# First four stages of a gather-and-multiply kernel picked out of whole tables by matmuls with ones and zeros

## Chip, cores and metric

The kernel runs on one core of a Trainium2 chip. The metric is the device time of one execution in microseconds (us), the median of several. All data are fp32, indices int32.

## What is computed

A batch of 2048 rows, each with 32 ids, one for each of 32 tables of 64 columns. The tables have 1000, 1250, 12500 or 125000 rows.

```
e     = stack(tbl_f[ids[:, f]])                      # (2048, 32, 64)
z     = sum(e, axis=-1)                              # (2048, 32)
outer = einsum('bpd,pde,bpe->bp', e[:, I], K, e[:, J])   # the 496 pairs i < j, K is (496, 64, 64)
h     = concat([z, outer, dense_ctx], axis=1)        # 32 + 496 + 16 = 544
h     = relu(h @ W_top1 + b_top1)                    # 512
h     = relu(h @ W_top2 + b_top2)                    # 256
y     = h @ W_top3                                   # (2048, 1)
```

## The kernel before

The batch is cut into NQ = 8 blocks of QB = 256 rows (two tiles of 128). The 32 fields are taken in pairs, from the last to the first: stage `a` of a block holds fields 2(15-a) and 2(15-a)+1, so stage 0 is fields 30 and 31. K is rearranged on the host and stays in SBUF as `k_sb` (8 MB).

The work on each engine is written out by hand, in an order fixed by tables:

- **POOL** gathers. One indirect DMA fetches 128 table rows (one field, one tile) into `gathered`, four a stage, 64 a block (L313 to L331). Four are in flight (`IN_FLIGHT`): before issuing gather k it waits for gather k-4 (`halve`, L302). From block 1 on `halve` also adds the two halves of each row for the sums z.
- **PE** turns a stage into `x_t` (fields along partitions, batch along columns) by two transposes into the one PSUM bank `tr` (`transpose`, L556); **ACT** copies `tr` into `x_t` (`keep_x`, L365). Everything that goes through `tr` goes one after the other: a fill waits until all earlier ones are kept (`free_tr`, `tr_kept`).
- The pairs are computed in 64 steps a block: 32 "even" steps (`multiply`, L635, K times x_t, weights from `k_sb`) and 32 "turned" ones (`multiply_turned`, L652, x_t as weights). DVE multiplies each result in PSUM by the other factor (`product`, L475; `turned_product`, L492). A turned product reads `gathered` directly, four stages (a block of COLS) at a time: the first ones need stages 4 to 7. The even products are summed by PE with a matrix of ones (`reduce`, L667), the turned ones by ACT (L427) or DVE (L521).
- In block 0 the order is: stages 0, 1, 2, even step 0, stages 3, 4, 5, even step 1, stage 6, even step 2, two turned steps (block 1 of stages), even 3 and so on; stage 7 before even step 5, stage 11 before step 12, stage 15 before step 25 (`FIRST_AHEAD`, L145). DVE sums each gathered stage over its 64 columns into `z_nat` (`sum_x`, L463); at the end of the block these are transposed (`sums_of_x`).
- **SP** loads: the ids, three small tensors, K in ten pieces (`K_LOADS`; from the fourth on each waits for a number of copies out of `tr`, L345), then w1 and w2, then for each block the dense columns in and the results out.
- ACT issues no DMA. The three layers on top (L583 to L633) run for block q-1 beside the steps of block q.

`x_t` has two blocks' slots (16 stages each), `z_sb` and `z_nat` two each.

Of the kernel before, what the change touches and what calls it, by code (L numbers as in the profile page):

```python
# [7 lines left out]
P = 128  # L8
NQ = 8
# [12 lines left out]
COLS = 4  # L22
YC = 4
# [98 lines left out]

STAGES_AT_ONCE = [1] + [2] * (NQ - 1)
# [82 lines left out]
def dlrm_tower(nc, ids, tables, kmat, dense_t, w1, b1, w2, b2, w3, out):  # L206
# [6 lines left out]
    with ctx:  # L213
# [23 lines left out]
        y_sb = sb("y_sb", [P, YN])  # L237
        idx = sb("idx", [P, NQ * STAGES * GATHERS], i32)
# [16 lines left out]
        small_loaded = sem("small_loaded")  # L255
        weights_loaded = sem("weights_loaded")
# [20 lines left out]
        LAST = NQ - 1  # L277
        FIRST_K = STAGES * GATHERS
# [14 lines left out]
        @block.gpsimd  # L293
        def _(pool):
            nc.gpsimd.memset(ident[:], 0.0).then_inc(zeroed, 1)
            pool.wait_ge(zeroed, 1)
            nc.gpsimd.affine_select(out=ident[:], in_=ident[:], compare_op=ALU.not_equal, fill=1.0,
                                    base=0, pattern=[[-1, P]], channel_multiplier=1).then_inc(consts_ready, 1)
            pool.wait_ge(idx_loaded, 16)


            def halve(k):  # L302
                G, n = divmod(k, GATHERS)
                t, f = divmod(n, 2)
                pool.wait_ge(gather_landed[k % IN_FLIGHT], (k // IN_FLIGHT + 1) * 16)
                if k < FIRST_K:
                    return
                if n == 0 and G - HR >= STAGES:
                    pool.wait_ge(x_summed, G - HR + 1)
                at = gathered[:, t, G % GR, f * D:(f + 1) * D]  # L310
                nc.gpsimd.tensor_tensor(x_half[:, G % HR, t, f, :], at[:, 0:D // 2], at[:, D // 2:D], ALU.add).then_inc(x_halved, 1)  # L311

            for k in range(NQ * STAGES * GATHERS):  # L313
                G, n = divmod(k, GATHERS)
                q, a = divmod(G, STAGES)
                t, f = divmod(n, 2)
                if k >= IN_FLIGHT:
                    halve(k - IN_FLIGHT)
                if n == 0 and G >= GR:
                    pool.wait_ge(tr_filled, place_of_stage(q - 1, a))  # L320
                    if q == 1:
                        pool.wait_ge(x_summed, G - GR + 1)
# [12 lines left out]
        @block.sync  # L335
        def _(sp):
# [27 lines left out]
        def _(act):  # L364
            def keep_x(q, a):  # L365
# [85 lines left out]
        def _(dve):  # L451
# [63 lines left out]
            def sum_turned(q, i):  # L515
                c, t = divmod(i, TILES)
                dve.wait_ge(prod_ready, q * NS + STEP_OF[q]["turned", i] + 1)
                if q >= 2:
# [4 lines left out]
                                        axis=AX.X, op=ALU.add).then_inc(summed_dve, 1)  # L523

# [23 lines left out]
        def _(pe):  # L548
# [20 lines left out]
            def sums_of_x(q):  # L569
                pe.wait_ge(x_summed, (q + 1) * STAGES)  # L570
# [221 lines left out]
```

## Time and profile before

| | us |
|---|---|
| median of 3 runs | 814.21 (813.42 to 814.73) |
| the profiled execution | 812.35 |
| its span on the core | 810.5 |
| busy: PE, DVE, ACT, POOL | 761.7, 720.8, 681.7, 607.3 |

The page of the profile gives one execution: busy time of each engine, the chain of waits that ended last, groups of instructions by line, and the DMA queues. Windows give the same for chosen stretches. The timeline lists instructions in order of time, like neighbours merged, with the idle time in front of each and who ended it. PE is TensorE's matmuls and PEld its weight loads; a matmul's end is modelled, so the distance from one start to the next says more than the duration. A fp32 matmul appears as two instructions, a transpose as one.

### The profile page before, as it was taken

How to read it: one execution, taken by the hardware profiler on the slowest of the kernel's cores; microseconds unless marked ns; L12 is line 12 of the kernel's file. 1: busy time of each engine (PE TensorE's matmuls, PEld its weight loads, DVE VectorE, ACT ScalarE, POOL GpSimd, SP SyncE). 2: the span in 40 equal slices, each digit the busy share in tenths (PEclk: the TensorE clock that was granted, in tenths of full speed). 3: DMA queues.
4: the chain of work that ended last, by engine and by line, in shares of the span. 5: the costliest groups of instructions: out<-in, count | busy, mean ns of one | idle time of the engine just before them, and what ended most of it. 6: DMA issues, size and time to landing. Idle time of an engine off the chain costs nothing.

```text
span 810.5 us, 20371 instructions
## 1 busy us (share of the span) xinstructions
PE 761.7 (94%) x6000; PEld 458.4 (57%) x6000; DVE 720.8 (89%) x684; ACT 681.7 (84%) x5282; POOL 607.3 (75%) x966
## 2 busy tenths in 40 slices
PE   0378989999999999999999999999999999999998
PEld 0144435565565666666666666656565665656656
DVE  0268999998999989999999989999999999999891
ACT  1057899989979999789989899799997899798993
POOL 6775888888888888888888888888868888660000
PEclk9999999999999999999999999999999999999999
DMA  4545111111111111111111111111111111110000
GB/s 136 162 134 181 27 24 26 25 26 25 26 26 25 26 25 25 26 25 25 25 27 25 25 25 26 25 25 26 24 23 24 26 25 26 20 21 2 1 2 1
DMA packets 20014, 28.74 MB, mean 35 GB/s; under 512 B 9024, under 2 KB 9664, under 8 KB 19008
## 3 DMA queue, kind: packets, MB, share of 16 engines
q0 software_dynamic: 16384, 16.81, 10.7%
q1 hardware_dynamic: 3520, 10.63, 4.0%
q8 instruction: 48, 0.79, 0.4%
q14 instruction: 62, 0.51, 0.2%
HBM read 27.40 MB, written 0.01 MB: 34 GB/s over the span
## 4 chain that ended last, share of the span: by engine, by line
PE 83%; DMA 6%; POOL 6%; issue 2%; ACT 2%; DVE 1%; DVEq 0%; POOLq 0%
PE m_ps L646 25%; PE m_ps L662 25%; PE acc L676 13%; PE tr L585 8%; DMA gathered<-in_tbl,idx 6%; POOL gathered L328 6%; PE tr L566 4%; PE tr L599 3%; ACT turned_act L427 1%; PE m_ps L648 1%; PE m_ps L585 1%; PE tr L580 1%; PE m_ps L599 0%; POOL x_half L311 0%; DMA idx<-in_ids 0%
## 5 line engine op out<-in xcount | busy, mean ns | idle before, releaser
L427 ACT ACTIVATE turned_act<-turned_act 128x64 f32<-128x64 f32 x2560 | 612.1, 244 | 26.3 <-DVE turned_act L513 26.2
L328 POOL DMA_INDIRECT gathered<-in_tbl,idx x512 | 489.4, 956 | 100.2 <-issue 74.4
L427 ACT ACTIVATION_READ_ACCUMULATOR turned_act<-turned_act 128x1 f32 x2560 | 486.4, 190 | 0.0
L488 DVE TENSOR_TENSOR prod<-m_ps,x_t 128x1024 f32<-128x1024 f32 x256 | 308.1, 1217 | 11.2 <-PE m_ps L648 10.7
L646 PE MATMUL m_ps<-x_t,k_sb 64*128 64x256 f32 x1024 | 271.8, 391 | 3.9 <-DVE turned_act L513 2.1
L648 PE MATMUL m_ps<-x_t,k_sb 64*128 64x256 f32 x1024 | 272.6, 392 | 0.0
L662 PE MATMUL m_ps<-k_sb,x_t 64*128 64x512 f32 x1024 | 262.7, 608 | 4.4 <-DVE turned_act L513 3.5
L646 PEld LDWEIGHTS m_ps<-x_t,k_sb 64*128 64x128 f32 x1024 | 182.4, 188 | 107.9 <-issue 63.2
L513 DVE TENSOR_TENSOR turned_act<-m_ps,gathered 128x1024 f32<-128x1024 f32 x160 | 193.4, 1217 | 25.0 <-PE m_ps L662 12.4
L648 PEld LDWEIGHTS m_ps<-x_t,k_sb 64*128 64x128 f32 x1024 | 182.1, 188 | 0.0
L662 PEld LDWEIGHTS m_ps<-k_sb,x_t 64*128 64x128 f32 x1024 | 92.6, 187 | 67.1 <-issue 43.7
L311 POOL TENSOR_TENSOR x_half<-gathered 128x32 f32<-128x32 f32 x448 | 117.2, 262 | 17.4 <-DVE z_nat L472 8.5
L676 PE MATMUL acc<-prod,sel 128*32 128x256 f32 x2048 | 123.6, 382 | 0.0
L513 DVE TENSOR_TENSOR turned_dve<-m_ps,gathered 128x1024 f32<-128x1024 f32 x96 | 117.0, 1219 | 3.2 <-POOL x_half L311 0.5
L521 DVE TENSOR_REDUCE z_turned<-turned_dve 128x16 f32<-128x1024 f32 x96 | 116.1, 1210 | 0.0
L371 ACT ACTIVATE x_t<-tr 128x512 f32<-128x512 f32 (+1 forms) x72 | 39.1, 543 | 66.7 <-PE tr L566 66.7
L676 PEld LDWEIGHTS acc<-prod,sel 128*32 128x32 f32 x2048 | 60.1, 110 | 54.0 <-issue 15.2
L566 PE MATMUL tr<-ident,gathered 128*128 128x128 f32 x256 | 45.3, 296 | 37.1 <-DMA gathered<-in_tbl,idx 37.1
L585 PE MATMUL tr<-z_sb,w_sb 128*128 128x256 f32 x280 | 67.9, 389 | 0.0
L566 PEld LDWEIGHTS tr<-ident,gathered 128*128 128x128 f32 x256 | 27.3, 144 | 70.2 <-issue 33.1
L585 PEld LDWEIGHTS tr<-z_sb,w_sb 128*128 128x128 f32 x280 | 50.9, 190 | 24.6 <-issue 18.8
L463 DVE TENSOR_REDUCE z_nat<-gathered 128x4 f32<-128x256 f32 x16 | 6.7, 416 | 31.8 <-DMA gathered<-in_tbl,idx 31.8
(36 smaller groups left out, 152.6 us busy)
## 6 DMA issues: line engine op xcount, KB each, us to landing
gathered<-in_tbl,idx POOLq DMA_INDIRECT x512, 2.5
k_sb<-in_kmat SPq DMA_DIRECT2D x7, 1024.0 KB, 4.9
w_sb<-in_w SPq DMA_DIRECT2D x1, 1280.0 KB
k_sb<-in_kmat SPq DMA_DIRECT2D x2, 256.0 KB, 3.1
k_sb<-in_kmat SPq DMA_DIRECT2D x1, 512.0 KB, 5.1
w_sb<-in_w SPq DMA_DIRECT2D x1, 512.0 KB
idx<-in_ids SPq DMA_DIRECT2D x1, 256.0 KB, 2.6
z_sb<-in_dense_t SPq DMA_DIRECT2D x8, 16.0 KB, 2.1
```

The source lines that it names most:

```text
L311: nc.gpsimd.tensor_tensor(x_half[:, G % HR, t, f, :], at[:, 0:D // 2], at[:, D // 2:D], ALU.add).then_inc(x_halved, 1)
L328: nc.gpsimd.indirect_dma_start(out=gathered[:, t, G % GR, f * D:(f + 1) * D], out_offset=None, in_=tables[2 * (STAGES - 1 - a) + f], in_of ...
L427: last = nc.scalar.activation(row, row, ACT.Copy, accum_out=z_turned[:, q % 2, t, 16 * c + n:16 * c + n + 1])
L488: nc.vector.tensor_tensor(prod[:, r % PR, :, :].rearrange("p u (e n) -> p u e n", e=2), m_ps[:, p % MR, :, :].rearrange("p u (e n) -> p u ...
L513: nc.vector.tensor_tensor(to, m_ps[:, p % MR, :, :], other, ALU.mult).then_inc(prod_ready, 1)
L521: nc.vector.tensor_reduce(z_turned[:, q % 2, t, 16 * c:16 * c + 16], turned_dve[:, (q * NTD + RANK[i]) % BD, :, :].rearrange("p f (u n) -> ...
L566: last = nc.tensor.transpose(tr[:, c, t * P:(t + 1) * P], gathered[:, t, (G + c) % GR, :], ident[:])
L585: last = nc.tensor.matmul(to, w1_sb[:, b, n * P:(n + 1) * P], z_sb[:, q % 2, b, :], start=(begin and b == blocks[0]), stop=(end and b == b ...
L646: nc.tensor.matmul(m_ps[:, p % MR, 0, n * QB:(n + 1) * QB], k_sb[0:D, at + n, :], x_t[0:D, slot(q, a0), :], start=True, stop=True)
L648: last = nc.tensor.matmul(m_ps[:, p % MR, 1, n * QB:(n + 1) * QB], k_sb[D:P, at + n, :], x_t[D:P, slot(q, a1), :], start=True, stop=True)
L662: last = nc.tensor.matmul(m_ps[:, p % MR, f, :], x_t[f * D:(f + 1) * D, slot(q, m), t * P:(t + 1) * P], k_sb[f * D:(f + 1) * D, at:at + CO ...
L676: last = nc.tensor.matmul(acc[c * 32:c * 32 + 32, 0:QB], sel[:, 30 - 2 * row:62 - 2 * row], prod[:, (q * NE + e) % PR, u, n * QB:(n + 1) * ...
```

## The change

Stages 0 to 3 of block 0 (fields 30 and 31 down to 24 and 25) are no longer gathered. Their tables all have 1000 or 1250 rows, that is 125 x 8 or 125 x 10. Each table is loaded whole, row 125-wise: partition p holds rows p*r to p*r+r-1 (r = 8 or 10), r times 64 columns. The 256 ids of a field are loaded to each of 125 partitions. For each c < r, DVE compares the ids with p*r + c (`rows_sb`), which gives a 125x256 matrix of ones and zeros, and PE multiplies the table's c-th 64 columns by it, adding up in `tr[f*64:(f+1)*64]`: the stage's x_t without a gather or a transpose. There are 18, 18, 16 and 18 such steps in the four stages, 70 in all, through a ring of five matrices (`HOT_RING`).

The loads (13 DMAs: the row numbers, then for each stage the ids and two tables) are issued by ACT at its start. Three stages' tables lie in the part of `x_t` that block 1 uses later; the fourth's and the ring lie in `w1_sb`, so SP's load of w1 now waits for the last pick. The ids lie in `z_sb`. The sums z of the four stages, which DVE took from `gathered`, are eight small matmuls on PE (`first_sums`, kept by ACT), placed before even step 2. POOL's gathers start with stage 4; their counts in all waits are shifted by K0 = 16.

```diff
+HOT = 4
+HOT_P = 125
+HOT_RING = 5
+TABLES_AHEAD = 3
...
+AHEAD[0, FIRST_AHEAD[HOT + 2]].append(("s", 0, 0))
...
+        hot_steps = [(a, c, f) for a in range(HOT) for c in range(max(HOT_R[a])) for f in range(2) if c < HOT_R[a][f]]
+        final = {(a, f): max(j for j, e in enumerate(hot_steps) if e[0] == a) for a in range(HOT) for f in range(2)}
+        used_by = [sum(i != final[hot_steps[i][0], 0] for i in range(j + 1)) for j in range(len(hot_steps))]
...
+        def hot_table(a, f):
+            home, first = (x_flat, 0) if a < TABLES_AHEAD else (w1_flat, TABLES_AHEAD)
+            at = D * (sum(sum(HOT_R[b]) for b in range(first, a)) + (HOT_R[a][0] if f else 0))
+            return home[0:HOT_P, at:at + D * HOT_R[a][f]]
...
-            for k in range(NQ * STAGES * GATHERS):
+            for k in range(K0, NQ * STAGES * GATHERS):
...
+            sp.wait_ge(tr_filled, place("x", 0, HOT - 1))
             sp.dma_start(w1_sb[:], w1.rearrange("(k p) n -> p k n", p=P)).then_inc(weights_loaded, 16)
...
+            act.dma_start(rows_sb[:], rows_hot).then_inc(rows_loaded, 16)
+            for a in range(HOT):
+                act.dma_start(hot_ids(a), ids_hot[a:a + 1, :].rearrange("o (f n) -> o f n", f=2).partition_broadcast(HOT_P)).then_inc(ids_hot_loaded[a], 16)
+                for f in range(2):
+                    act.dma_start(hot_table(a, f), tables[2 * (STAGES - 1 - a) + f].rearrange("(p r) d -> p (r d)", p=HOT_P)).then_inc(tables_loaded[a], 16)
...
+            def keep_first_sums():
+                act.wait_ge(tr_filled, place("s", 0, 0))
+                nc.scalar.activation(z_nat[:, 0, :, 0:2 * HOT], tr[:, 0, 0:TILES * 2 * HOT].rearrange("p (t n) -> p t n", t=TILES),
+                                     ACT.Copy).then_inc(tr_kept, 1)
...
+                if q == 0 and a < HOT:
+                    return
...
+            dve.wait_ge(rows_loaded, 16)
+            for j, (a, c, f) in enumerate(hot_steps):
+                if c == 0 and f == 0:
+                    dve.wait_ge(ids_hot_loaded[a], 16)
+                if j >= HOT_RING:
+                    i = j - HOT_RING
+                    if i == final[hot_steps[i][0], 0]:
+                        dve.wait_ge(tr_filled, place("x", 0, hot_steps[i][0]))
+                    else:
+                        dve.wait_ge(hot_used, used_by[i])
+                column = HOT_COLUMNS.index((HOT_R[a][f], c))
+                nc.vector.tensor_scalar(out=hot_matrix(j), in0=hot_ids(a)[:, f, :], scalar1=rows_sb[0:HOT_P, column:column + 1],
+                                        scalar2=None, op0=ALU.is_equal).then_inc(hot_ready, 1)
...
+            def pick_rows(a):
+                free_tr("x", 0, a)
+                pe.wait_ge(tables_loaded[a], 32)
+                for j, (b, c, f) in enumerate(hot_steps):
+                    if b == a:
+                        pe.wait_ge(hot_ready, j + 1)
+                        last = nc.tensor.matmul(tr[f * D:(f + 1) * D, 0, :], hot_table(a, f)[:, c * D:(c + 1) * D], hot_matrix(j),
+                                                start=(c == 0), stop=(c == HOT_R[a][f] - 1))
+                        if j == final[a, 0]:
+                            last.then_inc(tr_filled, 1)
+                        else:
+                            last.then_inc(hot_used, 1)
+
+            def first_sums():
+                free_tr("s", 0, 0)
+                for t in range(TILES):
+                    for a in range(HOT):
+                        at = 2 * (HOT * t + a)
+                        last = nc.tensor.matmul(tr[:, 0, at:at + 2], x_t[:, slot(0, a), t * P:(t + 1) * P], sel[:, 30:32],
+                                                start=True, stop=True)
+                last.then_inc(tr_filled, 1)
```

PE from its start to even step 1, before (`tr<-ident,gathered` are transposes, two a stage):

```order
L566 MATMUL tr<-ident,gathered 128x128 x6
L646 MATMUL m_ps<-x_t,k_sb 128x256
L648 MATMUL m_ps<-x_t,k_sb 128x256
L646 MATMUL m_ps<-x_t,k_sb 128x256
L648 MATMUL m_ps<-x_t,k_sb 128x256
L566 MATMUL tr<-ident,gathered 128x128 x6
L646 MATMUL m_ps<-x_t,k_sb 128x256
```

The same place in the changed kernel, up to even step 2 (`w_sb` is here `w1_sb` with ring and fourth table, `x_t` the first three stages' tables):

```order
L635 MATMUL tr<-w_sb,x_t 64x256 x52
L747 MATMUL m_ps<-x_t,k_sb 128x256
L749 MATMUL m_ps<-x_t,k_sb 128x256
L747 MATMUL m_ps<-x_t,k_sb 128x256
L749 MATMUL m_ps<-x_t,k_sb 128x256
L635 MATMUL tr<-w_sb 64x256 x18
L664 MATMUL tr<-ident,gathered 128x128 x4
L747 MATMUL m_ps<-x_t,k_sb 128x256
L749 MATMUL m_ps<-x_t,k_sb 128x256
L747 MATMUL m_ps<-x_t,k_sb 128x256
L749 MATMUL m_ps<-x_t,k_sb 128x256
L664 MATMUL tr<-ident,gathered 128x128 x2
L647 MATMUL tr<-sel,x_t 128x2 x8
```

Stages 0 to 3 are picks now, 52 before even step 0 and 18 behind it, and the small sums stand between stage 6 and even step 2.

DVE from the constants to the first turned product, before:

```order
L456 MEMSET z_sb 128x2x256
L463 TENSOR_REDUCE z_nat<-gathered 128x2x2 x3
L488 TENSOR_TENSOR prod<-m_ps,x_t 128x1024
L463 TENSOR_REDUCE z_nat<-gathered 128x2x2 x3
L488 TENSOR_TENSOR prod<-m_ps,x_t 128x1024
L463 TENSOR_REDUCE z_nat<-gathered 128x2x2
L488 TENSOR_TENSOR prod<-m_ps,x_t 128x1024
L513 TENSOR_TENSOR turned_act<-m_ps,gathered 128x1024
```

And in the changed kernel:

```order
L513 MEMSET z_sb 128x2x256
L595 TENSOR_SCALAR w_sb<-z_sb,rows_sb 125x256 x70
L547 TENSOR_TENSOR prod<-m_ps,x_t 128x1024
L522 TENSOR_REDUCE z_nat<-gathered 128x2x2 x2
L547 TENSOR_TENSOR prod<-m_ps,x_t 128x1024
L522 TENSOR_REDUCE z_nat<-gathered 128x2x2
L547 TENSOR_TENSOR prod<-m_ps,x_t 128x1024
L572 TENSOR_TENSOR turned_act<-m_ps,gathered 128x1024
```

All 70 comparisons stand ahead of the first product; four of the seven x sums are gone.

## Rows read from the trace of the kernel before

**Rows 1.** Page, part 4: the chain that ended last, by engine.

```profile
PE 83%; DMA 6%; POOL 6%; issue 2%; ACT 2%; DVE 1%; DVEq 0%; POOLq 0%
```

**Rows 2.** Windows: stretch, length; busy PE PEld DVE ACT POOL; granted clock; DMA share; GB/s.

```profile
40.00:50.00 10.00, 6.39 (x26) 3.60 (x26) 2.63 (x4) 0.38 (x1) 7.22 (x8) 1.00 0.56 189
60.00:70.00 10.00, 9.39 (x80) 5.12 (x80) 10.00 (x12) 7.36 (x59) 5.53 (x7) 1.00 0.91 329
70.00:80.00 10.00, 7.37 (x50) 4.35 (x54) 7.25 (x8) 6.62 (x54) 6.15 (x8) 1.00 0.25 66
100.00:140.00 40.00, 35.72 (x268) 18.11 (x266) 39.87 (x40) 37.37 (x300) 34.93 (x58) 1.00 0.13 25
200.00:700.00 500.00, 500.00 (x4026) 304.97 (x4024) 480.45 (x451) 454.52 (x3535) 428.23 (x703) 1.00 0.13 25
```

**Rows 3.** Timeline of DVE: start, duration, instruction, idle before and its releaser.

```profile
49.09 1.23 DVE L513 TENSOR_TENSOR turned_act<-m_ps,gathered 128x1024 f32<-128x1024 f32 x1 [2.47 <-PE m_ps L648]
50.23 1.21 DVE L513 TENSOR_TENSOR turned_dve<-m_ps,gathered 128x1024 f32<-128x1024 f32 x1
...
59.93 1.21 DVE L521 TENSOR_REDUCE z_turned<-turned_dve 128x16 f32<-128x1024 f32 x1
...
72.41 0.42 DVE L463 TENSOR_REDUCE z_nat<-gathered 128x4 f32<-128x256 f32 x1 [1.52 <-DMA gathered<-in_tbl,idx]
74.06 1.23 DVE L488 TENSOR_TENSOR prod<-m_ps,x_t 128x1024 f32<-128x1024 f32 x1 [1.23 <-PE m_ps L648]
```

**Rows 4.** Timeline: gathers on POOL, transposes of stages 11 and 15; last, gathers' landing.

```profile
3.67 1.10 POOL L328 DMA_INDIRECT gathered<-in_tbl,idx  x1 [2.20 <-DMA idx<-in_ids]
...
60.35 0.94 POOL L328 DMA_INDIRECT gathered<-in_tbl,idx  x1 [0.30 <-issue]
...
72.19 0.94 POOL L328 DMA_INDIRECT gathered<-in_tbl,idx  x1 [2.02 <-DMA gathered<-in_tbl,idx]
...
72.53 0.41 PE L566 MATMUL tr<-ident,gathered 128*128 128x128 f32 x2 [3.05 <-DMA gathered<-in_tbl,idx]
...
105.03 0.66 PE L566 MATMUL tr<-ident,gathered 128*128 128x128 f32 x4
...
DMA to landing us min/median/max: 2.3/2.5/7.0
```

**Rows 5.** Page, part 3: hardware queue's packets, MB, share; and two windows as in rows 2.

```profile
q1 hardware_dynamic: 3520, 10.63, 4.0%
...
4.00:6.00 2.00, 0.00 (x0) 0.00 (x0) 0.00 (x0) 0.00 (x0) 1.70 (x2) 1.00 0.97 262
46.00:48.00 2.00, 2.00 (x8) 0.86 (x6) 0.62 (x1) 0.00 (x0) 1.45 (x2) 1.00 0.98 411
```

**Rows 6.** Timeline of the start on DVE, ACT and PE; last, weight loads, page part 5.

```profile
0.83 0.11 DVE L452 MEMSET sel<- 128x62 f32 x1 [0.83 <-PEq L784]
...
10.92 1.28 ACT L371 ACT_TABLE_LOAD   x1 [10.92 <-PE tr L566]
12.21 0.38 ACT L371 ACTIVATE x_t<-tr 128x256 f32<-128x256 f32 x1
...
22.36 0.63 PE L646 MATMUL m_ps<-x_t,k_sb 64*128 64x256 f32 x1
...
22.78 0.63 PE L646 MATMUL m_ps<-x_t,k_sb 64*128 64x256 f32 x1
...
48.05 0.38 PE L646 MATMUL m_ps<-x_t,k_sb 64*128 64x256 f32 x1
...
48.26 0.38 PE L646 MATMUL m_ps<-x_t,k_sb 64*128 64x256 f32 x1
...
58.01 1.93 PE L676 MATMUL acc<-prod,sel 128*32 128x256 f32 x32
...
L676 PEld LDWEIGHTS acc<-prod,sel 128*32 128x32 f32 x2048 | 60.1, 110 | 54.0 <-issue 15.2
L585 PEld LDWEIGHTS tr<-z_sb,w_sb 128*128 128x128 f32 x280 | 50.9, 190 | 24.6 <-issue 18.8
```

More of the change, by code:

```diff
@@ L203, with dlrm_tower @@
 VECTOR_SUMS_BEHIND = (7, 10, 11, 12, 13, 15, 17, 18, 19, 23, 24, 25, 26, 27, 28, 29, 30, 31)
-def dlrm_tower(nc, ids, tables, kmat, dense_t, w1, b1, w2, b2, w3, out):
+SIZES = (125000, 1000, 1000, 1250, 12500, 1000, 1250, 12500, 1250, 1000, 12500, 1250, 125000, 125000, 12500, 12500,
+         1000, 12500, 1000, 1250, 1000, 12500, 12500, 1250, 1000, 1250, 1000, 1000, 1000, 1250, 1000, 1250)
+HOT_R = [[SIZES[2 * (STAGES - 1 - _a) + _f] // HOT_P for _f in range(2)] for _a in range(HOT)]
+HOT_COLUMNS = sorted({(_r, _c) for _pair in HOT_R for _r in _pair for _c in range(_r)})
+def dlrm_tower(nc, ids, ids_hot, rows_hot, tables, kmat, dense_t, w1, b1, w2, b2, w3, out):
     fp32, i32 = mybir.dt.float32, mybir.dt.int32
@@ L237, in dlrm_tower @@
         y_sb = sb("y_sb", [P, YN])
+        rows_sb = sb("rows_sb", [P, len(HOT_COLUMNS)])
         idx = sb("idx", [P, NQ * STAGES * GATHERS], i32)
@@ L255, in dlrm_tower @@
         small_loaded = sem("small_loaded")
+        rows_loaded = sem("rows_loaded")
+        ids_hot_loaded = [sem(f"ids_hot_loaded{a}") for a in range(HOT)]
+        tables_loaded = [sem(f"tables_loaded{a}") for a in range(HOT)]
+        hot_ready = sem("hot_ready")
+        hot_used = sem("hot_used")
         weights_loaded = sem("weights_loaded")
@@ L316, in _ @@
                 t, f = divmod(n, 2)
-                if k >= IN_FLIGHT:
+                if k >= K0 + IN_FLIGHT:
                     halve(k - IN_FLIGHT)
-                if n == 0 and G >= GR:
+                if n == 0 and G >= GR + HOT:
                     pool.wait_ge(tr_filled, place_of_stage(q - 1, a))
                     if q == 1:
-                        pool.wait_ge(x_summed, G - GR + 1)
+                        pool.wait_ge(x_summed, G - GR + 1 - HOT)
                     else:
@@ L496, in turned_product @@
                     for landed in gather_landed:
-                        dve.wait_ge(landed, (first + COLS) * GATHERS // IN_FLIGHT * 16)
+                        dve.wait_ge(landed, ((first + COLS) * GATHERS - K0) // IN_FLIGHT * 16)
                 elif t == 0:
@@ L554, in free_tr @@
                     pe.wait_ge(tr_kept, PLACE[what, q, n])
+            def pick_rows(a):
[18 more added lines that the diff above has]
+                last.then_inc(tr_filled, 1)
             def transpose(q, a):
                 G, n = q * STAGES + a, STAGES_AT_ONCE[q]
+                if q == 0 and a < HOT:
+                    pick_rows(a)
+                    return
                 if q == 0:
                     for landed in gather_landed:
-                        pe.wait_ge(landed, (G + n) * GATHERS // IN_FLIGHT * 16)
+                        pe.wait_ge(landed, ((G + n) * GATHERS - K0) // IN_FLIGHT * 16)
                 else:
@@ L613, in fill @@
                     transpose(q, n)
+                    return
+                if what == "s":
+                    first_sums()
                     return
@@ L769 @@
     w1_l[ZSHORT, SUM_ROWS:ZLAST] = w1_in[w1_in.shape[0] - DENSE:]
+    hot = [2 * (STAGES - 1 - a) + f for a in range(HOT) for f in range(2)]
+    assert all(inputs[f"tbl_{f}"].shape[0] == SIZES[f] for f in hot)
     arrays = {
+        "ids_hot": np.ascontiguousarray(ids[0:QB, hot].T).reshape(HOT, 2 * QB),
+        "rows_hot": np.array([[p * r + c for r, c in HOT_COLUMNS] for p in range(P)], np.float32),
         "ids": np.ascontiguousarray(ids_l).reshape(P, NQ * STAGES * GATHERS),
@@ L787 @@
     out = nc.dram_tensor("out_y", (1, B), mybir.dt.float32, kind="ExternalOutput").ap()
-    dlrm_tower(nc, aps["ids"], [aps[f"tbl_{f}"] for f in range(F)], aps["kmat"], aps["dense_t"],
+    dlrm_tower(nc, aps["ids"], aps["ids_hot"], aps["rows_hot"], [aps[f"tbl_{f}"] for f in range(F)], aps["kmat"], aps["dense_t"],
                aps["w1"], aps["b1"], aps["w2"], aps["b2"], aps["w3"], out)
```

20 lines of the change are left out of this document (15 added, 5 removed).

## Prediction

> **What bounds the kernel now.** I read the chain of waits first, then the windows, then the timeline of the first 75 us. The chain gives PE 83% of the span and DMA and POOL 6% each [rows 1]; nearly all of the DMA and POOL part lies before 115 us. The windows split the span in two. From 200 to 700 us PE is busy all the time and DVE 480 of 500 us, with POOL at 428 [rows 2]: what is gained or lost before that is neither made up nor given back there, and POOL has room. At the start it is different: DVE is busy 2.63 of 10 us from 40 to 50, 10.00 of 10 from 60 to 70, 7.25 in a dip from 70 to 80, and 39.87 of 40 from 100 to 140 us [rows 2]: where the chain names gathers after 80 us, DVE is full beside them, and an earlier gather alone would change nothing there. So the start ends at one event, the moment from which DVE is never idle. The timeline shows it: 49.09 us, the first turned product, which needed stage 7 gathered. Three even products (steps 0 to 2) lie before it [rows 3]. Behind it come only the two holes of the dip, 1.52 and 1.23 us, for the gathers of stage 11 [rows 3]. Before it everybody waits for gathers: POOL issues one in 0.94 + 0.30 = 1.25 us, and later in a stretch of heavy loads six of them take from 60.35 to 72.19, 1.97 us each [rows 4].
>
> So the number that I compare is the start of the first turned product with the same work behind it: 49.09 + 2.75 (holes that come later) = 51.8 us now.
>
> **What the change removes.** Sixteen of 64 gathers of the first block, 16 x 1.25 = 20 us of POOL at the least. Stage 7 is then ready after 16 gathers: between 3.67 + 16 x 1.25 + 2.5 = 26 us and, if every gather goes at the slow pace and lands after 7 us [rows 4], 42 us. Stage 11 comes after 32 gathers (at worst 74 us), stage 15 after 48 (105 us). PE transposed them at 72.53 (after 3.05 us of waiting) and 105.03 us [rows 4]; with the shift found below, and 2.75 us less waiting for the second, the need is at 75.7 (72.53 - 3.05 + 6.2) and 108.5 us. So the gathers stop being the bound nearly always and the dip of 2.75 us goes. The four x sums of DVE that go (0.42 us each) were in idle time: nothing. The w1 load waits for stage 3 picked; w1 is used first in block 1, so nothing, and the wait is passed already since K load 5 ahead of it waits for the same stage.
>
> **What it adds: loads.** Each of the four stages needs its ids, 125 rows of 2048 bytes, and two tables, 125 rows of 2048 or 2560: 0.832, 0.832, 0.768 and 0.832 MB. The price depends on how many of the 16 DMA engines carry them. No row shows a transfer of 125 rows. The nearest is a count: the hardware queue has 3520 packets [rows 5]. The data make 3104 of them (idx 128, three small loads 384, K 1280, w1 640, w2 512, eight dense loads of 16 rows 128, eight stores of 4 rows 32). The 416 left are 24 x 16 + 8 x 4: one closing packet for each engine used, 16 for transfers of 128 or 16 rows and 4 for those of 4 rows. So a transfer is dealt out in equal shares of rows. 125 is 5 x 25; in equal shares only 5 engines can have it. The ends are 16 engines and 5; I take **5**, as equal shares are what the count shows.
>
> By the Trainium skill (DMA: Bandwidth & Descriptors, "Why a DMA increments its semaphore by 16 and not by 1"), a hardware-queue transfer uses the largest number of engines up to 16 that divides the outermost counts of both sides, so 100 partitions go over 10. That rule speaks against this change: by it the sum is the one below, without it the 16-engine rival. The count of closing packets agrees for 4, 16 and 128 rows.
>
> An engine's rate: 262 GB/s / 16 = 16.4 GB/s in the first microseconds, 411 / 16 = 25.7 later [rows 5], 329 / 16 = 20.6 from 60 to 70 us [rows 2]. Stage 0: 0.832 / 5 + (0.262 idx + 1.049 first K) / 16 = 0.248 MB on each of the five engines: 9.6 to 15.1 us from about 2 us on, plus 0.5 to land: 12 to 17.6, I take **15 us**. Stages 1 to 3: 2.432 / 5 = 0.486 MB, at 25.7 GB/s 18.9 us; K load 3 (0.066 MB an engine) adds 2.5 and part of K load 4 1.5; gathers add 6% (2 KB an engine each 1.25 us): 24.3 us. Tables of stage 3 are there at **39.3 us** (36 with stage 0 early; 47.6 at the 20.6 rate with stage 0 late).
>
> **What it adds: picking.** 70 comparisons of 125x256 on DVE and 70 matmuls 125x64x256 on PE, 18, 18, 16, 18 a stage. DVE has no such operation; the upper bound is 0.35 us (products of 1024 start 1.14 apart [rows 3], less 768 elements at 1.03 ns, the slope between the x sum of 256 in 0.42 and the turned sum of 1024 in 1.21 [rows 3]); the lower 0.11, a memset of 62 elements [rows 6]. I take 0.3, near the upper, since that reads 256 elements too. On PE a 256-column instruction starts every 0.42 us at the slow clock (22.36, 22.78) and every 0.21 us at full clock (48.05, 48.26); a matmul is two of them [rows 6]. The granted clock reads 1.00 in both places; these spacings are its levels 1.2 and 2.4 GHz, and PE had been busy 2.00 of 2.00 us in the window before the second [rows 5]. The two fields of a stage fill different halves of PE's columns; the reduction, whose four column quarters go side by side (32 instructions in 1.93 us [rows 6]), says that a pair costs what one costs: 0.85 us slow, 0.43 full, and 0.6 where DVE sets the pace. A stage of ten such places is 5.7 us, 7.0 with a cold start; I take 6.3 for stage 3. The earlier stages hide under the loads: stage 0 ends at 15 + 7 + 1.9 (ACT's table load 1.28 and copy 0.38 [rows 6]) = 24, stage 1 at 30, stage 2 at 37. Picks end at 39.3 + 6.3 = **45.6 us**.
>
> **From there to the first turned product**, all in series through the one tr bank: copy of stage 3, 0.6; stages 4 and 5, transpose 0.5 and copy with its waits 0.6 each, 2.2; even step 1, 1.1; stage 6, 1.1; the new sums, 8 matmuls of two columns with 16 weight loads of 0.11 to 0.19 us (their means on the reduction and on layer 1 [rows 6]), 2.4 (1.8 to 4.6); even step 2, 1.1; its product 1.2: 9.7 us (8 to 12). So DVE is full from 45.6 + 9.7 = **55.3 us**, with the three even products behind it as before.
>
> **Sum**: 55.3 - 51.8 = +3.5 us. The profiled execution took 812.35 us (span 810.5); with the change 815.9. The median of the three runs is 814.21, so the forecast is **817.7 us**. The ends of the terms give 812.5 to 826 for this case.
>
> **Rivals.**
> (a) *All 16 engines carry the tables.* Then stage 0 is there at 9.5 us (2.14 MB at 262 to 411 GB/s) and picking is the bound: 9.5 + 7 + 1.9 + 5.7 + 0.6 + 4.8 + 0.6 + 0.9 (even step 0) + 5.7 = 36.7, full DVE from 46.4 us: 5.4 us faster, 808.8 (805.5 to 812). For it: all large loads here do so. Against it: 125 rows have no 16 equal shares. It decides below a landing of stage 3's tables at 35.8 us. Chance 0.23.
> (b) *The two fields' matmuls don't go side by side.* Stage 3 then costs 18 x 0.43 to 0.85, about 9 us: 820.5. Against it is the reduction's row. Chance 0.07.
> (c) *The comparisons hold POOL up.* POOL's issue takes 0.94 us at 60.35 beside a full DVE [rows 2, 4], but those DVE operations are products out of PSUM and sums. If each of the 70 delays a gather issue by its 0.3 us, stage 11 slips up to 20 us and a hole comes back: 826 to 830. Chance 0.06. The Trainium skill (SBUF — State Buffer, "Who interferes with whom") says that a tensor-with-scalar operation within SBUF can take the port pair that POOL shares, and then blocks it; no run here shows it yet.
> (d) *The loads go over 5 engines, yet the terms all fall short* and the first turned product comes at about 51.8 us: the change doesn't move the time, 814. Chance 0.06.
>
> **Numbers.** The forecast case has 0.58. Faster by over 0.2%: 0.20 from (a), 0.05 from the forecast's low end, 0.25. Within 0.2%, about what a measurement of this kernel can tell from no change: 0.06 from (d), 0.03 from (a), 0.09 from the forecast: 0.18. Slower: 0.57. The range that leaves out 2 in 10 at most takes in (a)'s middle and the forecast's slow end: 805.5 to 826. The likeliest case's own is 812.5 to 826.
>
> **What would show it.** Right: the tables' landings on ACT's queue about 7 us apart with a DMA share far under 1 while they run; closing packets of 5 for them; the last pick at 44 to 49 us; first turned product at 53 to 59; no idle DVE at 70 to 80; POOL's last gather some 20 us earlier against PE. Wrong: tables of stage 3 landed before 30 us (a); paired picks 0.43 us apart at full clock (b); POOL's 0.94 us longer while DVE compares (c); or DVE idle after 60 us for gathers or K, since five K loads and w1 now follow one another from 45 us on.

## Result, and the profile after

| | before | changed |
|---|---|---|
| median | 813.34 us (22 runs) | 815.63 us (22 runs) |
| ratio | | 1.0033, 95% interval 1.0022 to 1.0043 |
| profiled execution, its span | 812.35, 810.5 | 817.37, 815.6 |

The changed kernel is slower by 0.33%, 1.8 to 3.5 us. One of its 22 executions took 1987.27 us and is left out of the ratio. The forecast was slower, at 817.7 us, with a sum of +3.5 us.

The page of the changed kernel, parts 2 and 3 (queue, packets, MB, share), answers to [rows 5]:

```profile
PEclk9989999999999999999999999999999999999999
...
q1 hardware_dynamic: 3520, 10.63, 3.8%
q10 hardware_dynamic: 1704, 3.27, 1.1%
```

q10 is ScalarE's queue. Its loads carry 128 + 4 x 125 + 8 x 125 = 1628 data packets; the other 76 are 16 + 12 x 5. So each of the twelve transfers of 125 rows used exactly five DMA engines. The rule of the Trainium skill (DMA: Bandwidth & Descriptors, "Why a DMA increments its semaphore by 16 and not by 1"), the largest number up to 16 that divides the outermost counts of both sides, gives 5 for 125: the count agrees.

Timeline of PE in the changed kernel: start, duration, instructions, idle time before and who ended it. L635 are the picks, L664 transposes, L647 the first sums, L763 the first turned product.

```profile
16.09 7.18 PE L635 MATMUL tr<-w_sb,x_t 125*64 125x256 f32 x36 [16.09 <-DMA x_t<-in_tbl]
...
32.31 4.70 PE L635 MATMUL tr<-w_sb,x_t 125*64 125x256 f32 x32 [0.48 <-ACT x_t L421]
...
41.45 6.78 PE L635 MATMUL tr<-w_sb 125*64 125x256 f32 x36 [2.73 <-issue]
48.79 0.41 PE L664 MATMUL tr<-ident,gathered 128*128 128x128 f32 x2 [0.56 <-DMA gathered<-in_tbl,idx]
...
52.08 1.95 PE L647 MATMUL tr<-sel,x_t 128*128 128x2 f32 x16 [0.47 <-ACT x_t L421]
...
54.92 3.35 PE L763 MATMUL m_ps<-k_sb,x_t 64*128 64x512 f32 x8
```

Stage 0 cannot start before its tables are there (16.09), and PE stands for 2.73 us before stage 3 (41.45). The profile names no releaser for that idle time ("issue"). I take it for the wait for stage 3's tables, since it is gone in the kernel whose tables come early (e1b below). In between stands a cost that I had not seen. The timeline of ACT, whose queue (ACTq) issues the loads:

```profile
8.02 5.38 ACTq L411 DMA_DIRECT2D z_sb<-in_ids_hot  x1
13.43 4.77 ACTq L413 DMA_DIRECT2D x_t<-in_tbl  x2
...
20.52 3.89 ACTq L413 DMA_DIRECT2D w_sb<-in_tbl  x2
24.50 1.28 ACT L421 ACT_TABLE_LOAD   x1 [24.50 <-issue]
25.80 0.38 ACT L421 ACTIVATE x_t<-tr 128x256 f32<-128x256 f32 x1
```

One issue takes 5.38 us here and a pair of them 4.77, and ACT does nothing else meanwhile. Stage 0 was picked at 16.09 + 7.18 = 23.27, but ACT came to copy it 1.2 us later, after the last issue.

Timeline of DVE, answering to [rows 3]:

```profile
56.71 1.23 DVE L572 TENSOR_TENSOR turned_act<-m_ps,gathered 128x1024 f32<-128x1024 f32 x1 [0.35 <-PE m_ps L763]
58.32 1.23 DVE L572 TENSOR_TENSOR turned_dve<-m_ps,gathered 128x1024 f32<-128x1024 f32 x1 [0.38 <-PE m_ps L763]
```

The first turned product stands at 56.71 us instead of 49.09, and one hole of 0.38 us follows. In the windows, columns as in [rows 2], the dip from 70 to 80 us is gone; the middle of the span is what it was:

```profile
40.00:50.00 10.00, 7.42 (x40) 5.12 (x40) 6.09 (x16) 0.77 (x2) 6.60 (x7) 0.83 0.38 112
...
70.00:80.00 10.00, 9.91 (x84) 5.48 (x84) 10.00 (x11) 7.37 (x59) 6.90 (x9) 1.00 0.67 208
100.00:140.00 40.00, 35.63 (x238) 17.01 (x236) 39.87 (x39) 36.45 (x293) 30.42 (x50) 1.00 0.12 23
200.00:700.00 500.00, 500.00 (x3998) 305.29 (x3996) 480.26 (x449) 455.02 (x3543) 415.66 (x682) 1.00 0.12 24
```

And what POOL waited for in the first 60 us: total, times, longest; the changed kernel, then the kernel before.

```profile
POOL gathered L371 <- DMA gathered<-in_tbl,idx: 13.3, 17, 3.1
```

```profile
POOL gathered L328 <- DMA gathered<-in_tbl,idx: 3.4, 6, 0.7
```

The gathers that are left wait four times as long for landings. So the change takes 16 gathers away and the others wait more. The experiments had to say how much each side is worth.

### The profile page after: what moved, and what is told of

It reads as the page before. It is cut to its first block, busy times and chain, and to the rows that moved or that the text cites. A ratio compares the mean times of both kernels' runs of the same rounds, so it can differ in the third digit from the quotient of the medians.

```text
span 815.6 us, 20719 instructions
## 1 busy us (share of the span) xinstructions
PE 781.4 (96%) x6148; PEld 473.9 (58%) x6148; DVE 740.6 (91%) x750; ACT 681.8 (84%) x5283; POOL 592.5 (73%) x950
## 4 chain that ended last, share of the span: by engine, by line
PE 82%; DMA 6%; POOL 5%; issue 2%; ACT 2%; DVE 2%; DVEq 0%; POOLq 0%
PE m_ps L747 25%; PE m_ps L763 25%; PE acc L777 13%; PE tr L683 8%; DMA gathered<-in_tbl,idx 6%; POOL gathered L371 5%; PE tr L664 4%; PE tr L697 3%; ACT turned_act L484 1%; PE m_ps L749 1%; PE m_ps L683 1%; POOL x_half L354 1%; DVE turned_act L572 1%; PE tr L678 1%; DVE z_turned L580 0%
## 5 line engine op out<-in xcount | busy, mean ns | idle before, releaser
L371 POOL DMA_INDIRECT gathered<-in_tbl,idx x496 | 474.5, 957 | 100.6 <-issue 67.8
L747 PE MATMUL m_ps<-x_t,k_sb 64*128 64x256 f32 x1024 | 269.1, 388 | 2.5 <-DVE turned_act L572 0.8
L749 PE MATMUL m_ps<-x_t,k_sb 64*128 64x256 f32 x1024 | 269.8, 389 | 0.0
L763 PE MATMUL m_ps<-k_sb,x_t 64*128 64x512 f32 x1024 | 262.7, 608 | 4.4 <-DVE turned_act L572 3.5
L763 PEld LDWEIGHTS m_ps<-k_sb,x_t 64*128 64x128 f32 x1024 | 92.6, 187 | 66.2 <-issue 43.2
L664 PEld LDWEIGHTS tr<-ident,gathered 128*128 128x128 f32 x248 | 25.9, 141 | 32.3 <-issue 28.4
L595 DVE TENSOR_SCALAR w_sb<-z_sb,rows_sb 125x256 f32<-125x256 int32 x70 | 21.8, 377 | 23.8 <-PE tr L635 18.7
L664 PE MATMUL tr<-ident,gathered 128*128 128x128 f32 x248 | 42.0, 288 | 1.1 <-DMA gathered<-in_tbl,idx 1.1
```

Of the source, the lines that this page charges most:

```text
L371: nc.gpsimd.indirect_dma_start(out=gathered[:, t, G % GR, f * D:(f + 1) * D], out_offset=None, in_=tables[2 * (STAGES - 1 - a) + f], in_of ...
L664: last = nc.tensor.transpose(tr[:, c, t * P:(t + 1) * P], gathered[:, t, (G + c) % GR, :], ident[:])
L747: nc.tensor.matmul(m_ps[:, p % MR, 0, n * QB:(n + 1) * QB], k_sb[0:D, at + n, :], x_t[0:D, slot(q, a0), :], start=True, stop=True)
L749: last = nc.tensor.matmul(m_ps[:, p % MR, 1, n * QB:(n + 1) * QB], k_sb[D:P, at + n, :], x_t[D:P, slot(q, a1), :], start=True, stop=True)
L763: last = nc.tensor.matmul(m_ps[:, p % MR, f, :], x_t[f * D:(f + 1) * D, slot(q, m), t * P:(t + 1) * P], k_sb[f * D:(f + 1) * D, at:at + CO ...
```

## One number for every kernel

The prediction compared one quantity: the start of the first turned product plus the holes of DVE that come later (here up to 130 us). The traces of all undisturbed kernels give, in us:

| kernel | first turned | later holes | sum | span | span - sum |
|---|---|---|---|---|---|
| before | 49.09 | 2.75 | 51.84 | 810.5 | 758.7 |
| changed | 56.71 | 0.38 | 57.09 | 815.6 | 758.5 |
| e7 changed, again | 54.80 | 0.38 | 55.18 | 813.6 | 758.4 |
| e2b sums later | 51.84 | 1.44 | 53.28 | 811.6 | 758.3 |
| e8 filler | 56.82 | 0 | 56.82 | 815.1 | 758.3 |
| e4b loads alone | 55.35 | 4.98 | 60.33 | 819.5 | 759.2 |
| e1b 16 engines | 46.97 | 0.38 | 47.35 | 805.8 | 758.5 |
| e5 both | 42.70 | 1.44 | 44.14 | 802.5 | 758.4 |
| e6 ring of 28 | 40.41 | 1.98 | 42.39 | 801.1 | 758.7 |
| e9 other comparison | 42.60 | 5.18 | 47.78 | 806.9 | 759.1 |

Over a range of 18 us the last column moves by 0.9. So the place where the prediction looked is where the time of all these kernels is decided, and experiments can be read by their first 85 us.

One trace is one execution, though. The sums say +5.3 us for the changed kernel's trace and +3.3 for e7's, while the ratio of the executions says +2.7. The section on the clock takes up what is behind that.

## Experiments: how many DMA engines

One edit, only how the bytes are dealt out: ids to 128 rows, each table as 112 + 13 rows, which 16 and 13 engines can share.

```diff
-                act.dma_start(hot_ids(a), ....partition_broadcast(HOT_P))
+                act.dma_start(hot_ids_all(a), ....partition_broadcast(P))
-                    act.dma_start(hot_table(a, f), rows)
+                    act.dma_start(hot_table(a, f)[0:112], rows[0:112])
+                    act.dma_start(hot_table(a, f)[112:HOT_P], rows[112:HOT_P])
```

> The changed kernel with its loads cut so that 16 engines can share them: ids to 128 rows, each table as 112 rows plus 13 rows. Same bytes (ids 2% more). Theory A (the five-engine loads set the end of picking): tables of stage 0 land at 9 to 10 us instead of 16.1, those of stage 3 before 20; picking then is the bound, 9.5 + 7.2 + 2.9 + 5.6 + 0.5 + 4.7 + 0.5 + 1.5 + 6 = 38.4 us for the last pick instead of 48.2, first turned product at 47 instead of 56.7: 9 to 10 us faster than the changed kernel, about 5 faster than the kernel before (ratio 0.993 to 0.995). Rival B (picking and its handover bound it whatever the loads do): last pick after 45 us, within 3 us of the changed kernel (ratio to before 1.000 to 1.004).

The first four experiments (e1, e2, e3, e4) met a chip on which every kernel, the one before too, took some 1150 us at a mean granted clock of 0.89; in this experiment's trace the clock is 1.00 up to 30 us and 0.60 from 30 to 60. Only the first part of those traces says something. For this one: ratio 0.9962 (0.9921 to 1.0003), picks of stage 0 from 9.44 us. So it was run again.

> The kernel of e1_sixteen again, on another chip (the first chip ran every kernel, the one before too, at some 1150 us). There, up to 31 us, stage 0's tables were in use at 9.44 us and the copy of stage 2 began at 29.6, against 16.09 and 37.1 in the changed kernel. Theory A (five-engine loads): last pick near 38 us, first turned product near 47, 8 to 10 us faster than the changed kernel, ratio to before 0.992 to 0.995. Rival B (something behind the picks holds it): ratio 0.999 to 1.004.

Measured: 806.43 us against 810.84, ratio 0.994 (0.9916 to 0.9963). Timeline of PE:

```profile
9.36 7.30 PE L640 MATMUL tr<-w_sb,x_t 125*64 125x256 f32 x36 [9.36 <-DMA x_t<-in_tbl]
18.48 5.64 PE L640 MATMUL tr<-w_sb,x_t 125*64 125x256 f32 x36 [1.82 <-ACT x_t L426]
24.60 4.92 PE L640 MATMUL tr<-w_sb,x_t 125*64 125x256 f32 x32 [0.47 <-ACT x_t L426]
...
31.15 5.74 PE L640 MATMUL tr<-w_sb 125*64 125x256 f32 x36
```

Stage 0 comes 6.7 us earlier and stage 3 has no idle time before it: picking is the bound, not the loads. ACT's issues take 0.3 to 0.7 us each, although there are 21 instead of 13. The page counts 1952 packets on q10: 128 + 4 x 128 + 8 x 125 data and 16 + 4 x 16 + 8 x 16 + 8 x 13 = 312 closing ones. So the dealing out over five engines decides the sign: with it +2.7 us, without it -4.9 (0.6% of 810.8, 3.0 to 6.8). The prediction's rival (a) gave -5.4.

It works through the tables' landings and the picks behind them, and hardly through the gathers. POOL's waits in the first 60 us are, with 16 and 13 engines,

```profile
POOL gathered L374 <- DMA gathered<-in_tbl,idx: 11.2, 11, 3.1
```

against 13.3 with five and 3.4 before. Most of what the gathers lose goes with the loads however they are dealt out. ACT's long issues went with the same edit; no run separates them from the landings.

## Experiments: what the loads cost by themselves

The kernel before, with the twelve loads issued by ACT and used by nobody.

> The kernel before with the changed kernel's twelve loads of ids and tables added on ACT's queue and used by nobody. It measures what the loads take from gathers and K by themselves. Theory: the gathers are dealt over 16 engines and wait for the five busy ones, as POOL's waits for landings in the changed kernel show (15.8 us in 20 waits in the first 90 us against 9.0 in 10 before): stage 7 ready 2 to 5 us later than 49.1, time 2 to 5 us more than before (ratio 1.003 to 1.006). Rival: round robin between queues leaves the gathers alone, ratio 1.000.

> The kernel before with the changed kernel's twelve loads (ids and tables, 125 rows each) on ScalarE's queue and nothing that uses them: every stage is still gathered, nothing is picked. It leaves nothing of the computation out. Theory (the loads by themselves hold up the gathers: five engines of 16 are full and each gather waits for all 16): POOL's 16th, 28th and 32nd gathers are issued 5 to 8 us later than before (22.92, 38.51 and 43.76 us), the first turned product comes 5 to 8 us after 49.09, part of it is given back in the dip from 70 to 80 us, and the time is 4 to 8 us over before: ratio 1.005 to 1.010. Rival (the loads are hidden, and only the picks cost time): POOL's issues and the first turned product within 1 us of before, ratio 1.000 +- 0.002.

On the disturbed chip the ratio was 1.0012 (0.9956 to 1.0068), but in the part of the trace ahead of the slow-down the 16th, 28th and 32nd gathers were issued at 27.77, 46.64 and 51.63 us (before: 22.92, 38.51, 43.76). On the other chip: 820.04 us against 812.58, ratio 1.0086 (1.0058 to 1.0115). Timeline of DVE and a window:

```profile
55.35 1.23 DVE L545 TENSOR_TENSOR turned_act<-m_ps,gathered 128x1024 f32<-128x1024 f32 x1 [0.58 <-PE m_ps L694]
...
80.01 0.42 DVE L495 TENSOR_REDUCE z_nat<-gathered 128x4 f32<-128x256 f32 x1 [2.61 <-DMA gathered<-in_tbl,idx]
82.80 1.23 DVE L520 TENSOR_TENSOR prod<-m_ps,x_t 128x1024 f32<-128x1024 f32 x1 [2.37 <-PE m_ps L680]
```

```profile
30.00:40.00 10.00, 2.19 (x10) 1.03 (x6) 1.64 (x2) 0.38 (x1) 5.68 (x7) 1.00 0.91 292
```

From 30 to 40 us the DMA engines are busy 0.91 of the time (before: 0.51). POOL issues the same three gathers at 27.69, 46.23 and 51.23 us, the last 7.5 us later than before, and the first turned product is 6.3 us late, and the dip, which I expected to give some of it back, grew from 2.75 to 4.98 us. The rival "hidden" is out. The loads cost 0.86%, 7.0 us (4.7 to 9.3), and with the picks that use them the kernel is at +0.30% against the same executions of the kernel before (e7 below): picking instead of gathering gives back 814.80 - 820.04 = -5.2 us. So the change was never small; two large terms nearly cancel. The expectation's reason, that each gather waits for five full engines, is not shown: e1b's gathers wait 11.2 us beside loads over 16 and 13 engines. These loads by themselves over 16 engines were not run.

> The changed kernel without the table loads of stages 1 to 3: all four stages pick from the tables of stage 0 (that part of the computation is wrong), still on five engines. It leaves the picking chain alone after the first landing. Theory A: tables of stage 0 land a little earlier than 16.1 (ids of stage 1 right behind), and no wait for tables after that; last pick at 16.1 + 7.2 + 2.9 + 5.6 + 0.5 + 4.7 + 0.5 + 1.5 + 6 = 45.0 or a little earlier, 3 to 4 us faster than the changed kernel. If the landings of stages 1 to 3 cost nothing (rival B): under 1 us.

This kernel leaves out the tables of stages 1 to 3 and picks all four stages from those of stage 0. On the disturbed chip it took 1.006 (1.0011 to 1.0108) of the kernel before, and PE was slowed down before stage 2: no verdict. One reading stands ahead of that: its first picks start at 15.95 us, against 16.09 with all twelve loads. What is queued behind stage 0's tables hardly delays them.

## Experiments: the first sums and the clock

One line moves the first sums from before even step 2 to before even step 9.

```diff
-AHEAD[0, FIRST_AHEAD[HOT + 2]].append(("s", 0, 0))
+AHEAD.setdefault((0, 9), []).append(("s", 0, 0))
```

> The changed kernel with the eight small matmuls for the sums of stages 0 to 3 placed before even step 9 instead of even step 2. Theory: they stand in series in front of even step 2 (1.95 us of PE plus waits), and step 9 lies where PE waits for DVE. First turned product 2.0 to 2.5 us earlier, time 2 to 2.5 us less than the changed kernel, ratio to before about 1.000 to 1.001. Rival: the first turned product is then held by something else (turned matmuls at the slow clock) and under 1 us is gained.

> The kernel of e2_sums_later again, on another chip. Theory: the sums stand in series before even step 2; without them there the first turned product comes 2.0 to 2.5 us earlier than 56.7 and the time is 2 to 2.5 us below the changed kernel's, ratio to before 1.000 to 1.001. Rival: under 1 us.

Disturbed: 0.9876 (0.9808 to 0.9943), in a comparison whose executions scatter by 3%, and I lay nothing on it. On the good chip: 815.41 us, ratio 1.0049 (1.0031 to 1.0066). The trace shows the sums out of the way and the turned product at full clock:

```profile
50.46 1.88 PE L763 MATMUL m_ps<-k_sb,x_t 64*128 64x512 f32 x8
```

Its profiled execution is at 813.43 us; of its nine, four lie from 812.9 to 813.7 and five from 815.4 to 816.0. The trace has -1.9 us against e7, the medians have no gain. The first turned product itself comes 3.0 us earlier than in e7, but the moved sums leave DVE a hole later on (PE, then DVE):

```profile
64.90 1.95 PE L647 MATMUL tr<-sel,x_t 128*128 128x2 f32 x16
...
67.96 2.35 DVE L547 TENSOR_TENSOR prod<-m_ps,x_t 128x1024 f32<-128x1024 f32 x2 [1.44 <-PE m_ps L749]
```

So step 9 was not a place where PE had time to spare, as the expectation had it. What sets the two groups apart isn't settled, since only one execution has a trace.

With both edits:

> Both edits: loads over 16 engines and the sums before step 9. If the two terms are in series and independent, the gains add: 10 to 12.5 us below the changed kernel, ratio to before 0.989 to 0.992. If a later bound (gathers of stage 7 at 26 to 30 us at the earliest, or K) comes in, less than e1's gain plus 1.

803.93 us (803.46 to 804.85), ratio 0.9915 (0.9895 to 0.9936): faster than both kernels, and its mean granted clock is 1.000 in all six executions. Against e1b that is 2.5 us less by the medians, measured beside the same executions of the kernel before. Half of e1b's six executions are at a clock of 1.000 too, and their median is 804.60: against them e5 gains 0.7 us.

To see whether the lowered clock (0.83 in 40:50 above) is a part of the change's loss, twelve matmuls of the identity filled PE's idle time before stage 3.

```diff
+                if a == HOT - 1:
+                    for n in range(12):
+                        nc.tensor.matmul(tr[:, 0, 0:P], ident[:], ident[:], start=True, stop=True)
                 pe.wait_ge(tables_loaded[a], 32)
```

> The changed kernel once more, so that it and the three kernels below have the same chip and the same runs of the kernel before beside them. Expected from its first measurement: ratio to before 1.002 to 1.005. In the trace again: the first turned product on DVE at 56 to 57.5 us, the picks of stage 3 on PE from 41 to 42 us, the granted clock under 0.9 from 40 to 60 us. If the lowered clock belonged to that one execution and not to the kernel, it reads 1.00 there this time, and the first turned product comes 2 to 3 us earlier.

> The changed kernel with 12 matmuls of the identity by itself (128x128x128, results overwritten, about 2.6 us at full clock) on PE ahead of its wait for stage 3's tables, where it stood idle for 2.73 us. Theory (the lowered clock of 40 to 60 us is part of the loss and follows the idle stretch ahead of the picks): the granted clock reads 1.00 in 40:60, stage 3's 36 instructions of picks take 5.6 to 5.8 us instead of 6.78, the first sums and the turned product go at full clock (1.95 and 3.35 us become about 1.6 and 1.9), the first turned product comes 2 to 3 us earlier, at 53.5 to 54.5 us, and the time is 2 to 3 us under the changed kernel's on the same chip. Rival (the clock falls for another reason, or the landing of stage 3's tables and the chain of copies set the end by themselves): clock and the first turned product stay where they were, within 0.5 us, and the ratio is that of the changed kernel.

e7: 814.80 us against 812.58, ratio 1.003 (1.0016 to 1.0044). e8: 816.96, ratio 1.005 (1.0029 to 1.0072). PE in e7, then in e8:

```profile
40.58 5.58 PE L635 MATMUL tr<-w_sb 125*64 125x256 f32 x36 [1.41 <-issue]
...
52.85 3.52 PE L763 MATMUL m_ps<-k_sb,x_t 64*128 64x512 f32 x8
```

```profile
38.55 2.94 PE L634 MATMUL tr<-ident 128*128 128x128 f32 x24
41.58 5.72 PE L639 MATMUL tr<-w_sb 125*64 125x256 f32 x36
...
54.97 2.56 PE L767 MATMUL m_ps<-k_sb,x_t 64*128 64x512 f32 x8
```

The theory of the idle stretch fell. In e7 stage 3 is picked at full clock without any filler, so the slow picks of the profiled execution were its own; the filler only took 1 us more than the idle time that it filled. A slow stretch behind the first sums came in both, and it takes in the turned product (1.88 at full clock above). In windows, e7:

```profile
50.00:52.00 2.00, 2.00 (x18) 1.98 (x20) 0.76 (x2) 0.01 (x1) 1.35 (x2) 1.00 1.01 375
54.00:56.00 2.00, 2.00 (x6) 0.69 (x4) 1.48 (x2) 0.00 (x0) 0.94 (x1) 0.50 1.01 410
```

The changed kernel's first trace, e7, e8 and e1b, all with the sums ahead of even step 2, each have some 3.4 us (e1b 6.5) at a granted clock of 0.50, the lower of its two levels (1.2 and 2.4 GHz), that begin during the sums or up to 1.3 us after them. In e2b, e5 and e6, with the sums later, the clock reads 1.00 there, and behind the later sums too. In e9, which has them later too, it fell at 36 us, when PE had stood idle. What it costs at this place is small: in e7 DVE starts the first turned product 1.95 us after its matmuls began, in e2b 1.38, and the hole of 0.38 us comes on top, about 1 us in all. That the sums cause the fall is not shown. The kernel before has a slow turned product too, at a granted clock that reads 1.00:

```profile
45.14 3.07 PE L662 MATMUL m_ps<-k_sb,x_t 64*128 64x512 f32 x8
```

What the executions do show is what goes with the clock. Beside e7, e8, e4b and e9 the kernel before took 810.2 to 812.6 us in the nine executions whose mean granted clock was 1.000 (median 810.84) and 812.5 to 815.7 in the other ten (median 813.75). All twelve of e7 are at 0.998 or less, and their median is 814.80: 1.05 us above the ten, 4.0 above the nine. The other terms hardly depend on it: the loads by themselves cost 7.9 us at 1.000 and 7.4 below, the kernel with 16 engines (e1b, against its own executions of the kernel before) gains 5.0 and 5.2. So about half of the small loss goes with the changed kernel being always in the group of the lowered clock. Whether the change puts it there or that is another matter, no run settles.

## Experiments: comparisons and POOL

e6 is e5 with 28 matrices in the ring, so that DVE compares ahead and PE is no longer paced by it.

```diff
-HOT_RING = 5
+HOT_RING = 28
```

> The kernel of e5 with a ring of 28 matrices (kept in prod, slots 1 to 7) instead of 5, so that DVE compares ahead while tables land and stages change. Comparisons then run from 6 to about 27 us without a stop; a stage of picks costs PE 4.3 us at full clock (0.43 a pair) instead of 5.6: last pick at 32 to 34 instead of 38, 3 to 5 us below e5, ratio to before 0.983 to 0.988. If PE's pace in e5 is its own and not DVE's: no change against e5.

805.91 us, ratio 0.9939 (0.9918 to 0.9959): no better than e5, although its profiled execution (802.93) was. PE needs 4.54 us for the 18 picks of stage 3 instead of 5.74, but POOL stands still. POOL and DVE in e6:

```profile
15.06 0.94 POOL L375 DMA_INDIRECT gathered<-in_tbl,idx  x1 [0.30 <-issue]
18.71 8.46 POOL L375 DMA_INDIRECT gathered<-in_tbl,idx  x1 [2.71 <-DMA gathered<-in_tbl,idx]
```

```profile
12.03 14.32 DVE L601 TENSOR_SCALAR prod<-z_sb,rows_sb 125x256 f32<-125x256 int32 x52 [0.94 <-DMA z_sb<-in_ids_hot]
```

One gather instruction took 8.46 us instead of 0.94 and ended at 27.17, 0.82 us after the last of 52 comparisons without a pause (26.35). That is what rival (c) feared, in one piece instead of 0.3 us at a time. Is it the form of the comparison? The Trainium skill (SBUF — State Buffer, "Who interferes with whom") says that a tensor-with-scalar operation can take the port pair that POOL shares, and that one of two tensors has no such mode and, with both inputs in SBUF, contends only with POOL's reads; it reports that such an operation did not stall a DMA of POOL.

```diff
-nc.vector.tensor_scalar(out=hot_matrix(j), in0=hot_ids(a)[:, f, :], scalar1=rows_sb[..., column:column + 1], ...)
+nc.vector.tensor_tensor(out=hot_matrix(j), in0=hot_ids(a)[:, f, :], in1=rows_sb[..., column:column + 1].to_broadcast([HOT_P, QB]), ...)
```

> The kernel with 16 engines for the tables, the later sums and the ring of 28 matrices, with one edit: each comparison is a TENSOR_TENSOR of the ids with the row number spread over 256 columns, instead of a TENSOR_SCALAR. In the kernel without this edit 52 comparisons stood without a pause on DVE for 14.32 us (0.275 each), and one gather instruction on POOL that began inside it took 8.46 us instead of 0.94, ending as they ended. Theory (this form of comparison keeps POOL out): in the new form every gather instruction takes 0.94 to 1.1 us beside the comparisons; a comparison costs 0.30 to 0.40 us, so that the picks take up to 3 us more while the 1.66 us of waiting for a gather ahead of the second turned product go; time 1 us less to 2 us more than the kernel it is made from (ratio to before 0.992 to 0.997). Rival (any dense DVE work holds POOL up, or POOL stood for another reason): a gather instruction of 5 us or more again between 15 and 30 us.

808.72 us against 812.58, ratio 0.9954 (0.9935 to 0.9973). POOL and DVE:

```profile
19.00 11.46 POOL L375 DMA_INDIRECT gathered<-in_tbl,idx  x1 [2.63 <-DMA gathered<-in_tbl,idx]
30.77 0.94 POOL L375 DMA_INDIRECT gathered<-in_tbl,idx  x1 [0.30 <-issue]
```

```profile
12.07 17.58 DVE L601 TENSOR_TENSOR prod<-z_sb,rows_sb 125x256 f32<-125x256 int32 x52 [0.73 <-DMA z_sb<-in_ids_hot]
```

The theory fell: the other form holds POOL too, again until 0.81 us after its last (30.46 against 29.65). The page and this measurement differ, and the measurement decides. By the page's rule POOL's reads could be what waits; no run separates reads from writes. It isn't "any dense DVE work" either: in the changed kernel DVE is never idle from 70 to 80 us, mostly with products out of PSUM, and POOL does nine operations in 6.90 us there. In the changed kernel itself POOL's gathers took at most 1.10 us beside the comparisons, three of them during this stretch, in which the profile shows no pause either:

```profile
26.91 5.34 DVE L595 TENSOR_SCALAR w_sb<-z_sb,rows_sb 125x256 f32<-125x256 int32 x18 [3.10 <-PE tr L635]
```

Three gathers (12.56 to 15.06 us) also went through in 0.94 to 0.95 us in e6 while DVE was already comparing. In both places the comparisons start 0.30 us apart; while the gather stands in e6 they start 0.25 apart, but in e9 the pace is 0.33 us whether gathers pass or stand. What lets one gather pass and holds another is open.

## Why the prediction was right, point by point

Its mechanism held: one place decides, five engines carry the tables, and the last tables set the end of picking. The closeness of the number is in part luck, as the points say.

- **The place that decides**: right, by the last column of the table above, for ten executions.
- **Five engines**: right, by the closing packets, and decisive: with 16 and 13 the sign turns (e1b).
- **Loads**: stage 0's tables at 15 forecast, 16.1 measured; stage 3's at 39.3, and PE stopped waiting at 41.45 and 40.58 (e7).
- **Picks**: 6.3 us for stage 3, measured 6.78 and 5.58. The two fields go side by side: ten places in 5.6 us (rival (b) would have needed 9). 0.3 us a comparison: 18 in 5.34 us, the same. Last pick at 45.6, measured 48.2 and 46.2.
- **Handover** 9.7 us: from the last pick to the first turned product's start 8.5 and 8.6. The sums cost 1.95, forecast 2.4.
- **First turned product** at 55.3: 57.1 and 55.2 (e7), with the holes counted. That e7 meets it to 0.1 us is luck: tables 1.3 us later, picks 0.7 and handover 1.1 shorter, and a hole of 0.4 that I did not have.
- **Dip gone, gathers no longer the bound**: right, though by less room than it seemed. I gave the gathers' side no loss, and they waited 10 us longer (13.3 against 3.4); in the kernel before, where they are the bound, the same loads cost 7.0 us (e4b). The last gather of block 0 is still issued at 72.61 instead of 88.42.
- **Rival (c)**: comparisons can hold POOL up (e6, e9), but with the ring of five no gather instruction took over 1.10 us. Why not is open.
- **What was missed**: ACT as an issuer. I put the copies of stage 0 at 24 and gave the issues no time; they held ACT until 24.4, and the copy started at 25.8. It cost nothing at the end, since stage 3's tables came later still. It would have been a term with faster tables and the same slow issues.
- **The number**: 817.7 was 814.21 + 3.5. The ratio says +2.7 (1.8 to 3.5), 0.8 less; 0.9 more is the base, whose median was 813.34 this time. The sum started from a trace of the kernel before at a clock of 1.000 (812.35 us), the changed kernel was always below that, and no term stood for it.
- **The range**: its upper end, 826, leaves picking and handover at their middles. With 7.0 and 12 us for them it would be 829.

## What to carry to other kernels

Count the rows of a load before using it: these transfers over 125 partitions went over five DMA engines and landed late; splitting the tables as 112 + 13, with the ids to 128, turned a loss of 0.3% into a gain of 0.6%. Count also what added loads do to gathers beside them: POOL waited 11 to 13 us instead of 3.4, over five engines and over 16 alike. An engine that issues a long series of such loads isn't free until the last is issued. When a change moves the time little, measure its added traffic with nobody using it: here +7 us and -5 us stood behind +2. And when it moves the time by less than lies between executions of different mean clock (3 us here), compare executions of the same mean clock too.

## What the runs showed of the hardware

- An issue on ScalarE's queue took 0.3 to 0.7 us when the loads went over 16 and 13 engines, and up to 5.4 us when they went over five and stood one behind the other.
- One gather instruction on POOL took 8.46 us (e6) and one 11.46 us (e9) instead of 0.94 while DVE ran 52 comparisons within SBUF without a pause, in both forms of the comparison, and ended 0.8 us after the last of them. Not every gather beside such comparisons was held.
- Comparisons of 125x256 that wait for no semaphore start every 0.25 us as TENSOR_SCALAR (32 from 16 to 24 us in e6; 0.30 before that, while gathers pass) and every 0.33 us as TENSOR_TENSOR (43 from 14 to 28 us in e9).
- The closing packets of ScalarE's queue, 76 in the changed kernel and 312 in e1b, come out with 5 for a transfer of 125 rows, 16 for 128 and 112 rows and 13 for 13 rows.
